# A graph layer's own-feature transposition from rounded parts by unit-matrix products instead of a second normalisation

## The reference

```python
h = jnp.maximum(_layernorm(x, axis=-1), 0.0)          # x: 4096 x 256
deg = jnp.sum(adj, axis=1, keepdims=True) + 1e-05     # adj: 4096 x 4096, float32
h_neigh = (adj / deg) @ h
out = h_neigh @ W_neigh.T + b_neigh + h @ W_self.T + b_self
return x + jax.nn.relu(out)
```

## Time and profile before

| | us |
|---|---|
| median of 3 runs | 430.62 |
| lowest and highest | 427.32 and 432.87 |
| profiled execution, whole | 430.28 |
| its span, first to last instruction | 428.5 |
| PE busy | 414.2 |
| DVE busy | 377.5 |
| ACT busy | 207.6 |

### The profile page before, as it was taken

The page is one execution under the profiler, slowest core; times in us unless marked ns, Lnnn a source line. Parts: engine busy times, 40 slices in busy tenths (PEclk is TensorE's granted clock), DMA queues, the critical chain, the costliest instruction groups (busy, mean ns, idle before and its releaser), DMA issues.

```text
span 428.5 us, 5577 instructions
## 1 busy us (share of the span) xinstructions
PE 414.2 (97%) x2009; PEld 347.0 (81%) x2009; DVE 377.5 (88%) x459; ACT 207.6 (48%) x266; POOL 128.8 (30%) x113
## 2 busy tenths in 40 slices
PE   6999799998999989999999999999999999999995
PEld 5788588686888878889889888888888888888884
DVE  5999397899999897999899999979989899879954
ACT  4785474766443724735543543426343543426321
POOL 4778177494130307104104132005020222005020
PEclk9899989999999999999999999999999999999999
DMA  7899969989955357357437464644745366454401
GB/s 265 296 298 310 319 186 312 301 215 267 307 189 197 107 195 237 100 160 233 149 98 245 148 201 152 209 153 153 264 148 196 118 218 205 147 196 143 153 2 49
DMA packets 25483, 83.99 MB, mean 196 GB/s; under 512 B 2800, under 2 KB 4336, under 8 KB 25456
## 3 DMA queue, kind: packets, MB, share of 16 engines
q1 hardware_dynamic: 23152, 76.03, 52.4%
q0 software_dynamic: 2016, 7.34, 8.5%
q10 hardware_dynamic: 288, 0.26, 0.2%
HBM read 79.43 MB, written 4.19 MB: 195 GB/s over the span
## 4 chain that ended last, share of the span: by engine, by line
PE 71%; DVE 12%; DMA 8%; ACT 3%; issue 2%; POOL 2%; SPq 1%; DVEq 0%; ACTq 0%; POOLq 0%
PE banks L610 20%; PE banks L611 20%; PE banks L612 20%; PE banks L636 10%; DMA adj_raw<-adj_in 8%; DVE adj_lo L450 5%; DVE total L462 3%; ACT adj_hi L311 2%; PE banks L627 1%; DVE stats L413 1%; ACT h_row L314 1%; POOL rstd L227 1%; POOL shift L233 1%; PE banks L678 0%; DVE p_lo L491 0%
## 5 line engine op out<-in xcount | busy, mean ns | idle before, releaser
L311 ACT ACTIVATE adj_hi<-adj_raw 128x1024 fp32r<-128x1024 f32 x127 | 134.2, 1058 | 162.6 <-PE banks L612 108.6
L610 PE MATMUL banks<-adj_hi,h_hi 128*128 128x512 f32 x508 | 200.9, 396 | 6.6 <-DVE adj_lo L450 6.5
L611 PE MATMUL banks<-adj_hi,h_lo 128*128 128x512 f32 x508 | 199.0, 392 | 0.0
L612 PE MATMUL banks<-adj_lo,h_hi 128*128 128x512 f32 x508 | 198.4, 391 | 0.0
L450 DVE TENSOR_TENSOR adj_lo<-adj_raw,adj_hi 128x1024 fp32r<-128x1024 f32 x127 | 169.0, 1332 | 23.2 <-ACT adj_hi L311 22.6
L462 DVE TENSOR_TENSOR total<-total,adj_raw 128x1024 f32<-128x1024 f32 x106 | 131.2, 1238 | 0.0
L610 PEld LDWEIGHTS banks<-adj_hi,h_hi 128*128 128x128 f32 x508 | 96.0, 189 | 29.1 <-issue 8.2
L612 PEld LDWEIGHTS banks<-adj_lo,h_hi 128*128 128x128 f32 x508 | 96.0, 189 | 20.3
L611 PEld LDWEIGHTS banks<-adj_hi,h_lo 128*128 128x128 f32 x508 | 95.9, 189 | 18.7
L272 POOL TENSOR_TENSOR x_sb<-x_sb,own 128x1024 f32<-128x1024 f32 x7 | 30.6, 4375 | 127.5 <-ACT own L374 127.5
L266 POOL TENSOR_TENSOR own<-own,b_sum 128x1024 f32<-128x1024 f32 x8 | 31.7, 3961 | 111.2 <-ACT own L359 111.2
(11 more groups left out here) (72 smaller groups left out, 285.1 us busy)
## 6 DMA issues: line engine op xcount, KB each, us to landing
adj_raw<-adj_in SPq DMA_DIRECT2D x127, 512.0 KB, 3.8
total_dma<-adj_in POOLq DMA_DIRECT2D x14, 512.0 KB, 8.3
x_sb<-x_in SPq DMA_DIRECT2D x15, 256.0 KB, 7.3
rows_out<-x_sb SPq DMA_DIRECT2D x7, 512.0 KB, 5.0
adj_raw<-adj_in SPq DMA_DIRECT2D x2, 256.0 KB, 4.1
x_sb<-x_in SPq DMA_DIRECT2D x2, 128.0 KB, 2.3
w_raw<-w_neigh SPq DMA_DIRECT2D x1, 256.0 KB, 5.1
w_raw<-w_self SPq DMA_DIRECT2D x1, 256.0 KB, 6.1
```

Source lines behind the costliest of these rows:

```text
L311: nc.scalar.activation(adj_hi[:, r, :, :], adj_raw[:, r, :, :], ACT.Copy).then_inc(s_hi, 1)
L610: nc.tensor.matmul(bank, h_hi[:, j, feats], adj_hi[:, r, a, :], start=first, stop=False)
L611: nc.tensor.matmul(bank, h_lo[:, j, feats], adj_hi[:, r, a, :], start=False, stop=False)
L612: done = nc.tensor.matmul(bank, h_hi[:, j, feats], adj_lo[:, r, a, :], start=False, stop=last)
```

## The change

`make_h_again` is gone from ACT. `turn` now transposes `h_hi` itself: eight plain products with the rounded tile of h as the stationary operand and a 128 x 128 unit matrix of the rounded type (`unit`, made once from `ident` by ACT at step 28) as the moving one. ACT copies the two banks to `ht_hi` one step earlier than before, at `turn_at[q] + 3`. A new group `turn_low`, after the next unit on PE, waits for those copies, and does the same to `h_lo` into the same banks; ACT, not DVE, copies them to `ht_lo`, at `turn_at[q] + 4`. `turned_low` on DVE is gone. The two bias rows `b_raw` are loaded into the first half of `own`, which makes room for `unit`.

```diff
         own = sb("own", [P, UI, F])
+        b_raw = own[:, 0:2, :]
...
-        b_raw = sb("b_raw", [P, 2, F])
+        unit = sb("unit", [P, P], F32R)
...
-            def make_h_again(q):
-
-                if q == 0:
-                    act.wait_ge(s_hlo, T // 2)
-                else:
-                    act.wait_ge(s_turned, 2 * q)
-                for t in range(UI):
-                    last = normalise(q * UI + t, h_row[:, t // 2, t % 2, :])
-                last.then_inc(s_again, 1)
-
             def turned_high(q):
                 if q >= 1:
                     act.wait_ge(s_own, 2 * q)
                 for k in range(KC):
                     act.wait_ge(s_turned, 2 * q + k + 1)
                     nc.scalar.activation(ht_hi[:, k, :], banks[:, TURNED[k], :], ACT.Copy).then_inc(s_hthi, 1)
+
+            def turned_low(q):
+                for k in range(KC):
+                    act.wait_ge(s_turned_lo, 2 * q + k + 1)
+                    nc.scalar.activation(ht_lo[:, k, :], banks[:, TURNED[k], :], ACT.Copy).then_inc(s_htlo, 1)
...
+                if s == 28:
+                    act.wait_ge(s_ident, 1)
+                    nc.scalar.activation(unit[:, :], ident[:, :], ACT.Copy).then_inc(s_unit, 1)
...
                 for q in range(Q):
-                    if s == turn_at[q] + 1:
-                        make_h_again(q)
+                    if s == turn_at[q] + 3:
+                        turned_high(q)
                     if s == turn_at[q] + 4:
-                        turned_high(q)
+                        turned_low(q)
...
-            def turned_low(q):
-                for k in range(KC):
-                    dve.wait_ge(s_hthi, 2 * q + k + 1)
-                    nc.vector.tensor_tensor(ht_lo[:, k, :], banks[:, TURNED[k], :], ht_hi[:, k, :].bitcast(F32),
-                                            ALU.subtract).then_inc(s_htlo, 1)
...
             def turn(q):
-                pe.wait_ge(s_again, q + 1)
+
                 if q == 0:
-                    pe.wait_ge(s_ident, 1)
+                    pe.wait_ge(s_unit, 1)
                 else:
                     pe.wait_ge(s_htlo, 2 * q)
-                if q >= 1:
                     pe.wait_ge(s_deg, 3 * q)
                 for k in range(KC):
                     for t in range(UI):
-                        last = nc.tensor.transpose(banks[:, TURNED[k], t * P:(t + 1) * P],
-                                                   h_row[:, t // 2, t % 2, k * P:(k + 1) * P], ident[:, :])
+                        last = nc.tensor.matmul(banks[:, TURNED[k], t * P:(t + 1) * P], h_hi[:, q * UI + t, k * P:(k + 1) * P],
+                                                unit[:, :], start=True, stop=True)
                     last.then_inc(s_turned, 1)
+
+            def turn_low(q):
+
+                for k in range(KC):
+                    pe.wait_ge(s_hthi, 2 * q + k + 1)
+                    for t in range(UI):
+                        last = nc.tensor.matmul(banks[:, TURNED[k], t * P:(t + 1) * P], h_lo[:, q * UI + t, k * P:(k + 1) * P],
+                                                unit[:, :], start=True, stop=True)
+                    last.then_inc(s_turned_lo, 1)
...
                     if s == turn_at[q]:
                         turn(q)
+                    if s == turn_at[q] + 1:
+                        turn_low(q)
```

More of the change, by code:

```diff
@@ L136, in gnn_layer @@
         s_plo = sem("p_lo_ready")
-        s_again = sem("h_again_ready")
-        s_turned = sem("h_turned")
+        s_unit = sem("ident_rounded")
+        s_turned = sem("h_hi_turned")
+        s_turned_lo = sem("h_lo_turned")
         s_hthi = sem("ht_hi_ready")
@@ L553, in _ @@
                 for q in range(Q):
-                    if s == turn_at[q] + 4:
-                        turned_low(q)
                     if s == product_at[q]:
```

## The result

| | before | after |
|---|---|---|
| median, us | 430.64 | 434.15 |
| lowest and highest | 427.32, 432.87 | 433.70, 437.65 |
| profiled execution | 430.28 | 433.70 |
| block 0's turn begins, us | 107.75 | 104.77 |
| last product of the last unit begins, us | 420.56 | 423.98 |

The ratio of after to before is 1.0111, with a 95% interval of 1.0064 to 1.0158, from four executions of each: slower by about 1%, inside the 2% that count as no change. The changed kernel lost 6.4 us where the change acts, and its profiled execution won 3.0 us ahead of that place.

A forecast was written before the change was run, and what follows sets the result against it. PE was taken as the bound from 107.5 to 420.8 us. Removed turns -6.96, new products +14.46 and the hole -1.84 gave +5.7 us on 430.28, so 436.0 us; own range 434.5 to 438, wide range 430 to 441 us.

The forecast's parts named there:

- The bound: From 107.5 to 420.8 us PE is full, busy 311.73 of 313.30 us; time off ACT or DVE alone gains nothing.
- But one copy: Everything the change touches, except ACT's copy of `ident`, was said to lie in the middle stretch, 107.5 to 420.8 us.
- The price of a new product: In `turn` and `turn_low`: 128 added products of 128 columns on PE, 0.113 us each, 14.5 us in all.
- The rivals with 0.067 and 0.227 us: New products: weight loads hidden, 0.067 us each, 430.1 us, chance 0.09; or four passes, 0.227 us, 450.5 us, chance 0.13.
- The hole: PE's idle time at block 1, 151.2 to 152.79 us, traced to `make_h_again`; removing that was to save 1.84 us.
- no hole at 151 us: Sign that the prediction is right: PE no longer idles at block 1 around 151 us.
- The new wait on PE: `turn_low` waits for ACT's `ht_hi`: 2.4 us of slack in most blocks, block 0 tight, 0.2 us allowed.
- the 0.5 us that were to show the prediction right: Sign that the prediction is right: no PE wait for ACT's `ht_hi` above 0.5 us.
- ACT, DVE, own products, the copy: ACT loses 18.8 and gains 9.4 us, DVE loses 10.8; `ht_lo` comes earlier; copying `ident` takes 0.41 us: all priced at nothing.
- The sum: Whole kernel: -6.96 + 14.46 - 1.84 = +5.7 us, giving 436.0 us.
- the wide one: The forecast's wider range for the kernel's time, 430 to 441 us, leaving out four-pass products.
- another length of this stage: Sign that the prediction is wrong: a first stage, ahead of block 0's turn, other than 107.5 us long.

The follow-up runs named there:

- the layout run: The kernel before with only the change's memory layout and ACT's extra copy into `unit`, no product changed: 430.81 us, ratio 0.9998.

## Why the prediction was right, and where it was not

**The bound.** Right. PE was the bound over the whole stretch, and the doubled products came through one to one. "But one copy" was not exact: block 0's four second normalisations were on ACT from 103.26 us on, ahead of the stretch. PE did not wait there for them; its turn began 0.23 us behind the product ahead of it.

**The price of a new product.** Taken as 0.113 us between 0.109 and 0.120; measured 0.112. The reading behind it, that loads 0.11 us apart behind 16-column products would set the pace at 128 columns as well, held: 16 and 128 columns cost the same. The rivals with 0.067 and 0.227 us fell. Whether the load itself sets the pace or a fixed cost of each pair of load and product is open: every product here has a load of its own (PE x2073, PEld x2073). The Trainium skill's 81 ns for such pairs (page "TensorE: Matmul & The Clock Gate", section "Back-to-back issue gap") does not hold for these operands: 112 ns here.

**The hole.** The term came out and its reason did not. The prediction followed the hole back to the last wait, ACT's, and concluded that it would go with the normalisation. The runs show that it does not: without the normalisation it was 2.4 us of idle time, and with it put back into the changed kernel there was none. So the sign "no hole at 151 us" came true by luck. DVE is short of time at block 1, and POOL's add takes about 2.1 us from it. In the kernel before this fell into DVE's wait for ACT, so the trace named ACT; the wait cost DVE little that POOL would not have taken. In the changed kernel DVE still loses its time in `sums`, but PE arrives later:

```profile
139.88 6.76 POOL L274 TENSOR_TENSOR x_sb<-x_sb,own 128x1024 f32<-128x1024 f32 x1 [14.79 <-ACT own L371]
144.41 2.78 DVE L472 TENSOR_TENSOR sums<-total 128x512 f32<-128x512 f32 x1
...
148.58 1.22 DVE L450 TENSOR_TENSOR adj_lo<-adj_raw,adj_hi 128x1024 fp32r<-128x1024 f32 x1
150.70 0.39 PE L602 MATMUL banks<-adj_hi,h_hi 128*128 128x512 f32 x1
```

The unit was ready at 148.58 + 1.22 = 149.80 us and PE came at 150.70. From the start of block 0's turn PE takes 150.70 - 104.77 = 45.93 us to get there; in the kernel before it would have been there after 150.83 + 0.227 - 107.75 = 43.31 us, 2.6 us sooner. That is the added work: 0.02 for each of two turns, 0.70 + 1.04 for block 0's second group, 0.90 for block 1's. The added PE work filled the hole, and without `turn_low` it is back. The sum came out because that idle time was gone either way; of the new products, 1.84 us were free. The size of the term is that of one execution: the layout run, with the same PE work, had a hole half a microsecond smaller.

**The new wait on PE.** Right for seven blocks. For block 0 it was called tight and priced at 0.2 us; it cost 0.70 + 0.14 us, above the 0.5 us that were to show the prediction right. The split ahead of ACT's copy waits for a transfer, and the wait on PE, 0.70 us here, was 0.44, 1.05 and 1.14 us in the runs with 16 columns, in transposing mode and with the normalisation put back; a slack read as 0 was worth its spread and not 0.

**ACT, DVE, own products, the copy.** Right: 9.8 us less DVE work (377.5 to 367.7) and 7.1 us less on ACT (207.6 to 200.5) show nowhere in PE's time; there was no wait for `ht_lo`.

**The sum.** In the stretch: 16 x 0.90 + 0.84 - 8 x 0.88 - 1.84 = +6.4 us, and 6.39 were measured, against +5.7 predicted; the difference is block 0's wait. Against the stretch of the layout run it is 7.1 us. Whole executions showed +3.5 us between the medians: 434.15 us, 1.9 below the predicted 436.0 and just below its own range of 434.5 to 438, inside the wide one. The profiled one began its stretch 3.0 us earlier than that of the kernel before, in a stage that varies by 4.7 us over the profiles; the prediction had named another length of this stage as a sign against it. That the median came out so low is chance, as far as the runs show. The three later kernels with the same PE work (16 columns, transposing mode, normalisation put back) came out at 1.0147 to 1.0160, which is 6.3 to 6.9 us.

**Left open.** What makes the first stage long or short was not tried. Nor was a place for POOL's add that hides it without delaying the store, nor the kernel before with its normalisation kept and the add away from it, which would tell what the wait for ACT costs alone.

## What to carry to other kernels

When PE is full, count weight tiles, not columns: a rounded product of 16 columns here cost the same 0.11 us as one of 128, so replacing one transposition by two products doubled that bill, and the freed time on ACT and DVE paid nothing back. A wait that the trace names is the last of several: before pricing its removal, ask what else was going on while the waiting engine stood, because that work will be standing there next. And compare stretches that begin behind the noisy stage; here that turned a blurred 1% into 6.4 us that could be accounted for, and a stretch taken twice of the same work tells how far to trust it (0.7 us).

## What was not expected of the hardware

An add on POOL and DVE's instructions on SBUF shut each other out. POOL's add of 128 x 1024 recorded from 2.39 us (block 1's in the kernel before) to 7.25 us, the longer the later DVE left a gap; a two-element add recorded 4.55 us. A DVE instruction caught behind it took 2.8 in place of 0.7 us, or 3.4 in place of 1.2 us. It costs time only where DVE is behind: in the kernel before, block 3's add made an `adj_lo` of 3.40 us at 247.69 us, and PE did not wait. The Trainium skill, page "SBUF — State Buffer", section "SBUF: two separate sides", says that DVE and GpSimd share a port pair that one instruction holds to its end while the other blocks, among others where the DVE instruction has two inputs in SBUF and the GpSimd one reads SBUF, as `sums`, `adj_lo` and the add do. These runs agree, with about 2.1 us of DVE time for each such add that met it. The prediction did not look for it.
